# Moving the transposes of the next batches' input from step 1 to step 5 of a head pair

## What is computed

```python
q = (x @ Wq) ; k, v = split(x @ Wkv)            # 16 heads of 64
p = where(causal, exp(s - max(s)), 0)            # s = q k^T / 8, max over all keys
x = layernorm(x + ((p @ v) / (sum(p) + 1e-8)) @ Wo + bo)
xr, xk = mixes of x and x shifted by one token
x = layernorm(x + sigmoid(xr @ W_r.T) * (relu(xk @ W_k.T) ** 2 @ W_v.T))
```

## Time and profile before

| what | value |
|---|---|
| median of 3 runs | 1093.92 us (1092.81 to 1093.97) |
| the profiled execution | 1094.0 us |
| its span, first to last instruction | 1092.0 us |
| mean granted clock of TensorE | 0.993 |
| PE busy | 1033.6 us, 95% |
| DVE busy | 915.4 us, 84% |
| ACT busy | 746.6 us, 68% |
| POOL busy | 582.3 us, 53% |

### The profile page before, as it was taken

How to read it: one execution, slowest core, us unless ns; L and a number is a source line. 1 busy time by engine, 2 the same in 40 slices (tenths; PEclk the granted TensorE clock), 3 DMA queues, 4 the chain that set the end, 5 groups by cost and what they waited for, 6 DMA issues and landing times. The chain is left out here.

```text
span 1092.0 us, 22065 instructions
## 1 busy us (share of the span) xinstructions
PE 1033.6 (95%) x7427; PEld 673.6 (62%) x7427; DVE 915.4 (84%) x1546; ACT 746.6 (68%) x1709; POOL 582.3 (53%) x918
## 2 busy tenths in 40 slices
PE   7799999999999999999999999999999999999895
PEld 5565666666665666666666666666666666666563
DVE  5888888888887988888888888889888888898957
ACT  5766666666666666676666666666666766766767
POOL 5345655555564556566544556655555565554354
PEclk9999999999999999999999999999999999999998
DMA  5245555445555445555644455564445556554442
GB/s 162 69 111 123 136 141 123 117 111 125 134 124 136 118 109 122 131 123 136 146 113 106 114 134 123 139 145 118 115 114 126 132 126 146 123 124 117 115 106 77
DMA packets 74208, 134.05 MB, mean 123 GB/s; under 512 B 26864, under 2 KB 36848, under 8 KB 74096
## 3 DMA queue, kind: packets, MB, share of 16 engines
q1 hardware_dynamic: 73520, 132.26, 51.0%
q10 hardware_dynamic: 576, 0.39, 0.1%
HBM read 21.17 MB, written 2.36 MB: 22 GB/s over the span
## 5 line engine op out<-in xcount | busy, mean ns | idle before, releaser
L746 DVE TENSOR_SCALAR_CACHE_REDUCE tile<-ps_s 128x1024 f32<-128x1024 f32 x512 | 608.1, 1222 | 135.6 <-PE ps_s L984 128.0
L576 ACT ACTIVATE tile<-tile,neg_max 128x640 f32<-128x640 f32 (+7 forms) x512 | 396.2, 774 | 213.3 <-POOL tile L407 213.2
L984 PE MATMUL ps_s<-ks,qs 64*128 64x512 f32 x3072 | 424.2, 408 | 10.4 <-DVE tile L746 9.2
L407 POOL TENSOR_SCALAR_AFFINE_SELECT tile<-tile 128x128 f32<-128x128 f32 x512 | 149.7, 293 | 456.1 <-DVE tile L746 454.3
L984 PEld LDWEIGHTS ps_s<-ks,qs 64*128 64x128 f32 x3072 | 268.7, 184 | 129.3 <-issue 59.6
L1038 PE MATMUL ps_x<-pt,vs 128*64 128x256 f32 (+1 forms) x2560 | 270.2, 362 | 0.0
L755 DVE STREAM_TRANSPOSE stage<-tile 128x640 f32<-128x640 f32 (+3 forms) x256 | 255.2, 1026 | 0.0
L1038 PEld LDWEIGHTS ps_x<-pt,vs 128*64 128x64 f32 x2560 | 173.1, 137 | 109.3 <-issue 35.4
L997 PE MATMUL ps_x<-ident,tile 128*128 128x128 f32 x640 | 117.4, 290 | 26.5 <-ACT pt L624 15.8
L997 PEld LDWEIGHTS ps_x<-ident,tile 128*128 128x128 f32 x640 | 69.0, 140 | 107.0 <-issue 51.5
L918 PE MATMUL ps_x<-xs,ws 128*128 128x512 f32 x381 | 119.4, 423 | 0.6 <-DVE xs L721 0.4
(11 more groups left out here) (92 smaller groups left out, 579.2 us busy)
## 6 DMA issues: line engine op xcount, KB each, us to landing
pt<-stage SPq DMA_DIRECT2D x512, 120.0 KB, 2.4
pt<-stage SPq DMA_DIRECT2D x512, 88.0 KB, 2.1
rb<-recips SPq DMA_DIRECT2D x64, 256.0 KB, 4.0
y<-in_L_attn_x SPq DMA_DIRECT2D x3, 512.0 KB, 8.7
out<-y SPq DMA_DIRECT2D x3, 512.0 KB, 3.2
pt<-in_L_attn_Wkv SPq DMA_DIRECT2D x2, 384.0 KB, 6.8
pt<-in_L_attn_x SPq DMA_DIRECT2D x2, 256.0 KB, 4.5
wos<-in_L_attn_Wo SPq DMA_DIRECT2D x1, 512.0 KB, 7.1
```

Source lines behind the costliest of these rows:

```text
L407: pool.affine_select(out=block_of, in_=block_of, compare_op=ALU.is_ge, fill=fill, base=0, pattern=[[-1, P]], channel_multiplier=1).then_in ...
L576: act.activation(cols, cols, ACT.Exp, bias=neg_max[:, at:at + 1], scale=-1.0, accum_out=sums[:, p % 2, a, t:t + 1]).then_inc(s_exp, 1)
L746: dve.tensor_scalar(tile[:, at, :], ps_s[scores_at(p, t, a)][:, :], -SCALE, None, ALU.mult, ALU.min, accum_out=neg_max[:, at:at + 1]).then ...
L984: ins = mm(ps_s[scores_at(p, t, a)][:, c * HALF:(c + 1) * HALF], qs[rows, p % 2, qh, t * P:(t + 1) * P], ks[rows, p % 2, kh, c * HALF:(c + ...
```

## The change

`X_AT` goes from 1 to 5. The lists follow from it. PE makes the x transposes between the scores and `values` part 0 of step 5. ACT's two reads stand between the exponentials of tiles (5, 0) and (5, 1) instead of ahead of those of tiles (1, 0) and (1, 1). DVE's subtraction stands behind the block transposes of tiles (4, 0) and (4, 1), at the end of step 5, instead of between the evacuation of tile (1, 1) and a block transpose in step 1. The list of bank users puts x between ("out", p - 1, 0) and ("pv", p, 0).

```diff
-X_AT = 1
+X_AT = 5
...
                     if t in TURN_AT and t not in TURN_FIRST:
                         take_turned(p, TURN_AT[t], 0)
+                    if t == 4:
+                        take_turned(p, TURN_AT[t], 1)
+                    exp_of(p, t, 0)
                     if t == X_AT:
                         for b, c in x_half(p):
                             take_x(b, c)
-                    if t == 4:
-                        take_turned(p, TURN_AT[t], 1)
-                    exp_of(p, t, 0)
...
-                    if t == X_AT:
-                        for b, c in x_half(p):
-                            low_of_tokens(b, c)
                     if t == 1 and p > 0:
                         turn_tile(p - 1, TILES - 1, 0)
                     if t - 1 in BLOCKWISE:
                         turn_tile(p, t - 1, 0)
                         turn_tile(p, t - 1, 1)
+                    if t == X_AT:
+                        for b, c in x_half(p):
+                            low_of_tokens(b, c)
```

## The result

The changed kernel takes 1086.46 us, the median of 3 runs (1085.92 to 1087.09), where the kernel before took 1093.92. The ratio is 0.9937, 95% interval 0.9923 to 0.9951. The forecast was 1087.7 with a range of 1085.2 to 1090.0 and 0.92 on "faster", by which I meant more than 2.2 us. In a later comparison with more runs the same two kernels gave 0.9945 (0.9933 to 0.9958), which is 5.9 us by the medians 1093.12 and 1087.18. The profiled execution has a span of 1084.1 us, 7.9 less than before.

A forecast was written before the change was run, and what follows sets the result against it. PE, busy 95%, was the first suspect, but the movable price was 1.99 us per x pair, from PE waiting behind DVE. Giving back 1.99 less 0.94, six times, saves 6.3: 1094.0 to 1087.7 us, range 1085.2 to 1090.0.

The forecast's parts named there:

- What step 1 cost: DVE's 1.38 us wait for y and the subtraction's 0.61 delay PE in step 1; 1.99 us per x pair given back.
- PE's 0.59: The four x transposes, put before `values` part 0 in step 5, add 0.59 us to PE's gapless chain.
- The cover on DVE: In step 5, 1.57 us of block transposes cover the 1.38 us wait for y; the subtraction adds 0.61, parallel to PE.
- The new wait at part 1: In step 6, `values` part 1 waits for the subtraction: 0.35 us of wait, making it 0.94 late in all.
- The sum: Per x pair 1.99 us given back less 0.94 taken, 1.05; times six, 6.3 us.
- the clock as a rival: Behind the loop, an earlier start changes the half-clock stretch: up to 3.3 us less or more, 1084.4 or 1091.0; chance 0.05.
- The rule against it: Optimize the engine with highest occupancy first; PE's busy 1033.6 us don't change, so time would stay near 1094.0.

The follow-up runs named there:

- e2: The kernel before, with only DVE's subtraction moved behind the block transpose that follows it in step 1, x still there: 1084.90 us, ratio 0.9929.
- e1: The changed kernel with DVE's subtraction put in front of the two block transposes of step 5 instead of behind them: 1087.58 us, ratio 0.9954.
- e3: The changed kernel with DVE's subtraction made twice, the second signalling PE: 1090.26 us, ratio 0.9979.
- e5: The changed kernel measured once more, unaltered, with more runs: 1087.18 us, ratio 0.9945.
- e6: The kernel before, profiled once more, unaltered: 1094.80 us in one run.
- e10: The same code as e2, measured again on one chip with e9: 1085.71 us, ratio 0.9929.
- e9: The changed kernel, unaltered, measured again on one chip with e10: 1087.17 us, ratio 0.9943.

## Why the prediction was right

**What step 1 cost** was the uncovered wait for y plus the subtraction, in front of an evacuation that PE waits for. This is confirmed by e2, which takes away 1.28 of the 1.97 by order alone. Steps 1 to 3 of the x pairs are now those of plain pairs.

**PE's 0.59** was measured as 0.59 (316.14 to 316.73).

**The cover on DVE** held: no idle in front of the subtraction, evacuation (6, 0) 0.61 late where I had 0.59. e1 shows that the cover is the transposes. I would have overrated it: without it the price goes up by 0.26, not by the 0.65 of my expectation, because y holds the subtraction back to about the same moment either way, and DVE has slack at the end of the pair.

**The new wait at part 1** exists, and e3 shows it. Its size is the term that was off: part 1 is 0.87 late in place of 0.94. The subtraction started 1.49 us after the transposes' start, before their recorded end, where I had counted 1.59, and took 0.66, not 0.69. The profile doesn't name it as I said it would: it stands under "issue", with 0.18 us of idle on PE where I had said 0.35.

**The sum** of 6.3 us against 6.4 us in the loop was right: the 1.05 per pair was 1.10, which is 6.6 in all, and the plain pairs took 0.2 back. The median came out 1.2 us under the forecast, and the reason lies behind the loop, where the sum had counted on no change.

**Behind the loop** I had the clock as a rival with 0.05 and at most 3.3 us. Its sign, the pairs as said and another time behind the loop, came up beside the main forecast. Its price is 1.2 us in the mean between 6.8 and 3.4 us of half clock, and about 0.2 between 3.4 and none. The same code shows either length, so it scatters from execution to execution; that starting the stage earlier also makes a short stretch likelier is neither shown nor excluded. The scatter is large enough to explain why the first comparison gave 7.5 us by the medians and the next two 5.9 and 6.2, though only one execution of each was profiled. By the Trainium skill, TensorE: Matmul & The Clock Gate, "What's actually happening", the gate's observation isn't tied to the kernel's start; the two profiles of the same code with 3.4 and 6.8 us agree with that. The length goes with the moment at which the stretch begins, as the figures of e5 and e6 above say; what sets that moment in one execution stays open.

**The rule against it** (the Trainium skill, Perfetto Trace Analysis, "Identifying the Most-Contended Engine"), as I had applied it, did not hold here: PE's busy time is 1033.0 against 1033.6 us, and the kernel is 0.6% faster. I had left out half of it: the same section of the Trainium skill says that the headroom of TensorE is judged by MFU (its share of the peak FLOP rate) and by the busy share of its weight loads, and not by matmul busy time. That busy share is 62% here, under DVE's 84%, and read so the rule doesn't speak for PE (MFU was not measured). The gain lay in PE's gap behind DVE. To look for such gaps is what the Trainium skill, Perfetto Trace Analysis, "Optimization Strategy", says.

## What to carry to other kernels

When a side job crosses three engines, look in each in-order queue for work that can stand in front of its waiting instruction: here a swap of two DVE instructions within the step was worth 7.7 us of loop time, more than the move to another step. Then look at who inherits the buffer: with banks used in turn, a moved user changes the predecessor of the two behind it, and that, not the moved work, made most of the difference between steps 5, 6 and 7. Take the effect of such a change from the lengths of the repeated pieces, which agree to 0.05 us in the kernel before and to 0.14 at worst where no stretch of half clock reaches into one, before the total, which scatters by over 1 us.

## What the runs showed of the hardware

A stretch at 1.2 GHz behind the loop costs far less than its length, and not in proportion to it: 3.4 us of it made the next stage 0.6 us late and left about 0.2 us at the end, 6.8 us made it 2.2 late in e10 and left 1.1 to 1.5 in the five executions that had it. A part of the delay is taken back by a DVE mix of 1024 columns, which took 2.02 us in e9 and 1.53 and 1.26 where it started later. A DVE subtraction of 512 columns that reads PSUM started 0.08 us before the recorded end of the transposes in front of it (320.12 against 318.63 + 1.57 = 320.20).
